# Storing the last step of a scan in eight half-tile stores on two issuing queues instead of two stores on one

## The chip, the cores and the metric

The kernel runs on one core of a Trainium2 chip. The metric is the time of one execution on the device, in microseconds (us). A core has a matrix engine (TensorE, PE in the profile, with its weight loads listed as PEld), a vector engine (VectorE, DVE), an activation engine (ScalarE, ACT), GpSimd (POOL), and SyncE (SP), which here only waits and issues transfers (DMAs). Each engine has its own instruction queue that it works through in order; engines wait for each other through semaphores. A DMA is issued by one engine's queue, carried out by 16 DMA engines, and counts 16 on a semaphore when it has landed.

## The reference

The input is x of shape (4, 512, 32, 48) in float32. It is group-normalised (32 groups of channels), and the result f is scanned over its last axis, forward and then backward, with one 512 by 512 matrix Wc (the centre tap of the convolution weight):

```
step(prev, x_i):  y = Wc @ prev + b;  y = where(y >= 0, y, a*y);  cur = y + x_i
fl  = forward scan over w = 0 .. 47        (47 steps after the first column)
out = backward scan over w = 46 .. 0       (47 steps, starting from fl[47])
result = x + out
```

So there are 94 dependent steps, each a 512x512 by 512x128 product (128 columns are 4 images by 32 rows) followed by a bias, a leaky ReLU and an addition. Column 0 of the output is known only after the last of them.

## The kernel before

The 512 channels are four tiles of 128 partitions. A step j computes four output tiles o = 0..3. For each, PE accumulates four matmuls (one per input tile k), 16 in all (L338, order in `UNITS`, so that tile o = 0 is finished before the others), ACT makes `above` = relu(z + b) (L406) and `below` = relu(-z - b) (L408), and DVE adds `above` to the state (L487, "part") and then subtracts a times `below` (L492, "whole"), which counts `state_ready`. The next step's matmuls wait for `state_ready` tile by tile.

In the backward half each finished column w gets the input added on DVE (L534 in the loop, L543 for columns 3, 2 and 1, which are written into places of `state` that are free) and is stored by SyncE, one DMA of 256 KB per column (L236), each after a wait on `out_ready`. The input of column 0 has been added ahead, before the backward half starts (L546), so the last step's tiles are final when L492 has run. That last step (`LAST_ORDER`) does part and whole of tile 0, then of tile 1, and so on.

Column 0 ("step 0" in the change) is stored in two pieces from SyncE: tiles 0 to 2 together after `state_ready` shows three tiles (L238, L239; 192 KB), tile 3 after the fourth (L240, L241; 64 KB). Then SyncE waits for the first three columns' stores (L242) and for all others (L243), and the kernel ends once every engine has met at the closing barrier (L59). The output tensor has the layout (W, 128, 4, 128): in column 0 a partition's four tiles are contiguous, 512 bytes each.

ACT issues one DMA in the whole kernel, at its start: the 2.5 KB of parameters (L349). Its 94 steps run in a loop (L401 to L411), after which its queue has nothing left but the closing barrier.

Of the kernel before, what the change touches and what calls it, by code (L numbers as in the profile page):

```python
# [9 lines left out]
P = 128  # L10
# [26 lines left out]
APART = 3  # L37
# [6 lines left out]

def scan_program(nc, x, w, par, out):
    KT, N, _, W, H = x.shape
    COLS = N * H
    FEAT = KT * COLS
    C = KT * P
    FWD = W - 1  # L50
    STEPS = 2 * FWD
# [7 lines left out]
    with ExitStack() as ctx:  # L59
        def sb(name, shape):  # L60
            return ctx.enter_context(nc.sbuf_tensor(name, shape, F32))

        def sem(name):
            return ctx.enter_context(nc.semaphore(name))

        xin = sb("xin", [P, KT, N, W, H])
        state = sb("state", [P, W, KT, COLS])
# [34 lines left out]
        def gmean(t):  # L102
            return gsums(t)[:, 0]

        def gvar(t):
            return gsums(t)[:, 1]

        def gdev(t):
            return spread(t, 4, P)[:, 0]
# [4 lines left out]
        def pieces(b):  # L114
            return PIECES.get(b, [W])
# [36 lines left out]
        state_ready = sem("state_ready")  # L152
        out_ready = sem("out_ready")
        input_added = sem("input_added")
        early_stored = sem("early_stored")
        stored = sem("stored")

        SROW, XROW = W * FEAT, NBLK * BLK

        def reg(eng, value, low, high):  # L160
            return value if isinstance(value, int) else eng.snap(value, min_val=low, max_val=high)
# [21 lines left out]
        def loop(eng, first, last, body):  # L183

            n = (last - first) // 2
            if n > 1:
                with eng.Fori(0, n) as turn:
                    for u in range(2):
                        body(turn * 2 + (first + u), (first + u) % 2)
                first += 2 * n  # L190
            for j in range(first, last):
                body(j, j % 2)

        def units(b):

            found = []
            begin = 0
            mine = BY_ACT.get(b, (0, 0))
            for i, size in enumerate(pieces(b)):
                w0 = begin  # L200
                begin += size
                while w0 < begin:
                    by_act = w0 == mine[0] and mine[1] > 0
                    w1 = mine[1] if by_act else w0 + UNIT
                    assert w1 <= begin
                    found.append((w0, w1, i, by_act))
                    w0 = w1
            return found

        def record(b, i):  # L210

            return sum(1 if by_act else 2 for _, _, _, by_act in units(b)[:i])

        def x_part(b, w0, w1):
            return xin[:, b // N, b % N, w0:w1, :].rearrange("p w h -> p (w h)")
# [7 lines left out]
        @block.sync  # L223
        def _(sp):
            for b in range(NBLK):
                w0 = 0
                for i, size in enumerate(pieces(b)):
                    sp.dma_start(xin[:, b // N, b % N, w0:w0 + size, :],  # L228
                                 x[b // N, b % N, :, w0:w0 + size, :]).then_inc(x_loaded[b][i], 16)
                    w0 += size  # L230
            for k in range(KT):
                sp.dma_start(w_t[:, k, :], w[k * P:(k + 1) * P, :]).then_inc(w_loaded[k], 16)
            for i in range(FWD):
                step = W - 1 - i
                sp.wait_ge(out_ready, i + 1)
                sp.dma_start(out[step], free[step] if step in free else state[:, step, :, :]).then_inc(  # L236
                    early_stored if i < APART else stored, 16)
            sp.wait_ge(state_ready, 4 * (STEPS - 1) + KT - 1)  # L238
            sp.dma_start(out[0, :, 0:KT - 1, :], state[:, 0, 0:KT - 1, :]).then_inc(stored, 16)  # L239
            sp.wait_ge(state_ready, 4 * STEPS)  # L240
            sp.dma_start(out[0, :, KT - 1, :], state[:, 0, KT - 1, :]).then_inc(stored, 16)  # L241
            sp.wait_ge(early_stored, 16 * APART)  # L242
            sp.wait_ge(stored, 16 * (FWD - APART + 2))  # L243

        @block.tensor
        def _(pe):
# [100 lines left out]
        @block.scalar  # L347
        def _(act):
            act.dma_start(params[:, :], par[:, :]).then_inc(params_loaded, 16)  # L349
            act.wait_ge(counts_set, 4)  # L350
            junk = state[:, W - 2:W, :, :].rearrange("p w k c -> p (w k c)")

            def unit_stats(nth):
                b = act_blocks[nth]
                i, (w0, w1, piece, _) = next((i, u) for i, u in enumerate(units(b)) if u[3])
                rec = bstat[:, b, record(b, i), :]
                size = (w1 - w0) * H
                act.wait_ge(x_loaded[b][piece], 16)
                nc.scalar.activation(junk[:, 0:size], x_part(b, w0, w1), ACT.Identity, scale=1.0 / size,  # L359
                                     accum_out=rec[:, 1:2]).then_inc(act_step, 1)  # L360
                act.wait_ge(act_step, nth + 1)
                nc.scalar.activation(junk[:, 0:size], x_part(b, w0, w1), ACT.Square, scale=-1.0, bias=rec[:, 1:2],  # L362
                                     accum_out=rec[:, 2:3]).then_inc(act_stats, 1)
                act.wait_ge(act_stats, nth + 1)

            def square_deviations(t):
                k, n0, n1 = BATCHES[t]
                act.wait_ge(dev_done, t + 1)
                nc.scalar.activation(dev2[:, k, n0:n1], gdev(t)[:, :, 0], ACT.Square).then_inc(dev2_done, 1)  # L369

            def group_values(t):
                k, n0, n1 = BATCHES[t]
                act.wait_ge(gvar_done, t + 1)
                nc.scalar.activation(var_eps[:, k, n0:n1], gvar(t)[:, :, 0], ACT.Identity,  # L374
                                     bias=eps[:, 0:1]).then_inc(var_done, 1)
                nc.scalar.activation(mean[:, k, n0:n1], gmean(t)[:, :, 0], ACT.Identity).then_inc(mean_kept, 1)

            unit_stats(0)
            act.wait_ge(params_loaded, 16)
            nc.scalar.mul(negative[:, :], params[:, :], -1.0).then_inc(negated, 1)  # L380
            unit_stats(1)
            unit_stats(2)
            square_deviations(0)
            group_values(0)
            unit_stats(3)
            unit_stats(4)
            square_deviations(1)
            group_values(1)
            unit_stats(5)
            unit_stats(6)  # L390
            square_deviations(2)
            group_values(2)
            unit_stats(7)
            unit_stats(8)
            square_deviations(3)
            act.wait_ge(gshift_done, 1)
            nc.scalar.activation(shift[:, :], gshift[:, :, 0], ACT.Identity).then_inc(shift_kept, 1)
            group_values(3)
            act.wait_ge(negated, 1)

            def body(j, par):  # L401
                nth = [reg(act, j * 4 + (o + 1), 1, 4 * STEPS) for o in range(KT)]
                for o in range(KT):
                    act.wait_ge(tile_done, nth[o])
                    z = psum[:, 4 * par + o, 0:COLS]
                    nc.scalar.activation(above[:, par, o, :], z, ACT.Relu, bias=params[:, o:o + 1],  # L406
                                         scale=1.0).then_inc(above_done, 1)
                    nc.scalar.activation(below[:, par, o, :], z, ACT.Relu, bias=negative[:, o:o + 1],  # L408
                                         scale=-1.0).then_inc(below_done, 1)

            loop(act, 0, STEPS, body)  # L411

        @block.vector
        def _(dve):
# [228 lines left out]
```

## Time and profile before

| | |
|---|---|
| median of 3 runs | 377.96 us (377.90 to 378.09) |
| profiled execution, its own time | 378.02 us |
| its span, first to last instruction | 376.5 us |
| PE busy in the span | 351.9 us (93%) |
| DVE, ACT busy | 287.2 us, 228.1 us |
| granted TensorE clock | 1.000 (2.4 GHz) |
| last state tile written | 374.24 us |
| last store issued, landed | 374.27 us, about 375.9 us |

The span is what the profile resolves; the 1.5 us between it and the execution's own time lie outside of any instruction. The chain of waits names, walking back from the last instruction, what released each piece of work. The DMA issue rows give the size of each DMA and the time from its issue to its landing.

### The profile page before, as it was taken

How to read it: one execution, taken by the hardware profiler on the slowest of the kernel's cores; microseconds unless marked ns; L12 is line 12 of the kernel's file. 1: busy time of each engine (PE TensorE's matmuls, PEld its weight loads, DVE VectorE, ACT ScalarE, POOL GpSimd, SP SyncE). 2: the span in 40 equal slices, each digit the busy share in tenths (PEclk: the TensorE clock that was granted, in tenths of full speed). 3: DMA queues.
4: the chain of work that ended last, by engine and by line, in shares of the span. 5: the costliest groups of instructions: out<-in, count | busy, mean ns of one | idle time of the engine just before them, and what ended most of it. 6: DMA issues, size and time to landing. Idle time of an engine off the chain costs nothing.

```text
span 376.5 us, 10084 instructions
## 1 busy us (share of the span) xinstructions
PE 351.9 (93%) x3096; PEld 350.3 (93%) x3096; DVE 287.2 (76%) x927; ACT 228.1 (61%) x803; POOL 19.3 (5%) x30
## 2 busy tenths in 40 slices
PE   0269999999999999999999999999999999999996
PEld 0169999999999999999999999999999999999995
DVE  2678997887888878655656778778778787787786
ACT  3765556566565565665665655656656656556564
POOL 2177000000000000000000000000000000000000
PEclk9999999999999999999999999999999999999999
DMA  7998000000000000000000112212212212122122
GB/s 304 423 412 311 2 0 0 1 0 0 1 0 0 1 0 0 0 0 0 0 0 0 57 67 74 84 56 84 84 56 84 78 62 84 64 76 84 56 111 84
DMA packets 10808, 26.30 MB, mean 70 GB/s; under 512 B 1328, under 2 KB 1584, under 8 KB 10800
## 3 DMA queue, kind: packets, MB, share of 16 engines
q1 hardware_dynamic: 10656, 26.22, 18.0%
q14 instruction: 6, 0.05, 0.0%
q8 instruction: 2, 0.03, 0.0%
q10 hardware_dynamic: 144, 0.00, 0.0%
HBM read 13.63 MB, written 12.58 MB: 70 GB/s over the span
## 4 chain that ended last, share of the span: by engine, by line
PE 90%; DMA 6%; SPq 2%; DVE 1%; ACT 0%; issue 0%; ACTq 0%
PE psum L338 88%; DMA xin<-in_x 6%; SPq L228 2%; PE psum L293 1%; PE psum L303 1%; DVE state L436 0%; DVE state L492 0%; DVE state L487 0%; ACT state L359 0%; PE psum L267 0%; ACT state L362 0%; PE psum L286 0%; ACT above L406 0%; PE psum L262 0%; PE psum L284 0%
## 5 line engine op out<-in xcount | busy, mean ns | idle before, releaser
L338 PE MATMUL psum<-state,w_t 128*128 (+1 forms) x2976 | 332.7, 275 | 0.0
L338 PEld LDWEIGHTS psum<-state,w_t 128*128 128x128 f32 x2976 | 332.5, 192 | 0.1
L406 ACT ACTIVATE above<-psum,params 128x128 f32<-128x128 f32 x376 | 140.1, 373 | 132.3 <-PE psum L338 128.8
L487 DVE TENSOR_TENSOR state<-above,state 128x128 f32 (+1 forms) x376 | 108.4, 288 | 66.7 <-ACT above L406 65.4
L408 ACT ACTIVATE below<-psum,negative 128x128 f32<-128x128 f32 x376 | 140.4, 374 | 0.0
L492 DVE SCALAR_TENSOR_TENSOR state<-below,negative,state 128x128 f32 (+1 forms) x376 | 123.6, 349 | 7.1 <-DVE state L487 0.2
L534 DVE TENSOR_TENSOR state<-state,xin (+1 forms) x45 | 30.8, 684 | 0.0
L418 DVE BATCH_NORM_STATS2 bstat<-xin 128x6 f32<-128x512 f32 x33 | 21.1, 678 | 12.3 <-DMA xin<-in_x 12.3
L436 DVE TENSOR_SCALAR state<-xin,mean,rstd 128x320 f32<-128x320 f32 (+3 forms) x73 | 28.6, 439 | 0.0
L254 PE MATMUL psum<-chan,centre 128*128 128x64 f32 (+1 forms) x8 | 2.0, 348 | 17.9 <-DVE chan L432 17.9
L254 PEld LDWEIGHTS psum<-chan,centre 128*128 128x128 f32 x8 | 1.6, 255 | 18.1 <-issue 13.5
L359 ACT ACTIVATE state<-xin 128x1024 f32<-128x1024 f32 (+1 forms) x9 | 8.2, 913 | 4.7 <-DMA xin<-in_x 4.6
L293 PE MATMUL psum<-same_group 128*128 128x128 f32 x56 | 9.3, 339 | 0.0
L362 ACT ACTIVATE state<-xin,bstat 128x1024 f32<-128x1024 f32 (+1 forms) x9 | 9.1, 1006 | 0.3
L293 PEld LDWEIGHTS psum<-same_group 128*128 128x128 f32 x56 | 9.0, 252 | 0.0
L596 POOL TENSOR_TENSOR state<-xin,mean 128x512 f32<-128x512 f32 x6 | 6.2, 1041 | 0.4
L601 POOL TENSOR_TENSOR state<-state,rstd 128x512 f32<-128x512 f32 x6 | 6.2, 1041 | 0.4
L586 POOL TENSOR_TENSOR rstd<-var_eps,minus_half 128x4 f32<-128x4 f32 (+2 forms) x5 | 4.5, 895 | 17.1 <-ACT var_eps L374 16.7
L267 PEld LDWEIGHTS psum<-dev,same_group 128*128 128x128 f32 x8 | 1.6, 249 | 3.6 <-ACT dev L369 3.6
L267 PE MATMUL psum<-dev,same_group 128*128 128x64 f32 (+1 forms) x8 | 2.3, 374 | 2.8 <-ACT dev L369 2.8
L359 ACT ACT_TABLE_LOAD x1 | 1.3, 1283 | 5.6 <-DMA xin<-in_x 5.6
L303 PE MATMUL psum<-state,w_t 128*128 128x128 f32 x32 | 4.2, 280 | 0.2 <-DVE state L436 0.2
(38 smaller groups left out, 26.2 us busy)
## 6 DMA issues: line engine op xcount, KB each, us to landing
out_y<-state SPq DMA_DIRECT2D x47, 256.0 KB, 2.0
xin<-in_x SPq DMA_DIRECT2D x13, 768.0 KB, 12.7
xin<-in_x SPq DMA_DIRECT2D x7, 256.0 KB, 17.7
w_t<-in_w SPq DMA_DIRECT2D x4, 256.0 KB, 10.3
xin<-in_x SPq DMA_DIRECT2D x1, 512.0 KB, 19.6
out_y<-state SPq DMA_DIRECT2D x1, 192.0 KB, 1.9
out_y<-state SPq DMA_DIRECT2D x1, 64.0 KB, 1.6
params<-in_par ACTq DMA_DIRECT2D x1, 2.5 KB, 4.9
```

What stands on the lines that cost most here:

```text
L293: nc.tensor.matmul(idle, same_group[:, :], same_group[:, :], start=True, stop=True)
L303: mm = nc.tensor.matmul(psum[:, o, 0:COLS], w_t[:, k, o * P:(o + 1) * P], state[:, 0, k, :], start=k == 0, stop=k == KT - 1)
L338: mm = nc.tensor.matmul(psum[:, 4 * par + o, 0:COLS], w_t[:, k, o * P:(o + 1) * P], xs[k], start=k == 0, stop=k == 3)
L359: nc.scalar.activation(junk[:, 0:size], x_part(b, w0, w1), ACT.Identity, scale=1.0 / size, accum_out=rec[:, 1:2]).then_inc(act_step, 1)
L362: nc.scalar.activation(junk[:, 0:size], x_part(b, w0, w1), ACT.Square, scale=-1.0, bias=rec[:, 1:2], accum_out=rec[:, 2:3]).then_inc(act_s ...
L406: nc.scalar.activation(above[:, par, o, :], z, ACT.Relu, bias=params[:, o:o + 1], scale=1.0).then_inc(above_done, 1)
L408: nc.scalar.activation(below[:, par, o, :], z, ACT.Relu, bias=negative[:, o:o + 1], scale=-1.0).then_inc(below_done, 1)
L418: return nc.vector.bn_stats(bstat[:, b, record(b, i):record(b, i) + 2, :].rearrange("p r v -> p (r v)"), x_part(b, w0, w1))
L436: return nc.vector.tensor_scalar(state[:, w0:w1, k, n * H:(n + 1) * H], xin[:, k, n, w0:w1, :], mean[:, k, n:n + 1], rstd[:, k, n:n + 1], ...
L487: nc.vector.tensor_tensor(sts[o], above[:, par, o, :], sts[o], ALU.add).then_inc(part_done, 1)
L492: nc.vector.scalar_tensor_tensor(sts[o], below[:, par, o, :], negative[:, KT:KT + 1], sts[o], ALU.mult, ALU.add).then_inc(state_ready, 1)
L534: return nc.vector.tensor_tensor(place, place, ready(dve, xin_step(dve, step)), ALU.add)
```

## The change

Column 0 is stored tile by tile. For each of its four tiles SyncE stores partitions 0 to 63 and ScalarE's queue stores partitions 64 to 127, each after a wait for that tile's `state_ready`. ScalarE's four waits and four DMAs come after its loop, so behind all of its activations, and count on a new semaphore, `last_stored`, for which SyncE waits at the end. No other engine's instructions change.

```diff
+        last_stored = sem("last_stored")
...
-            sp.wait_ge(state_ready, 4 * (STEPS - 1) + KT - 1)
-            sp.dma_start(out[0, :, 0:KT - 1, :], state[:, 0, 0:KT - 1, :]).then_inc(stored, 16)
-            sp.wait_ge(state_ready, 4 * STEPS)
-            sp.dma_start(out[0, :, KT - 1, :], state[:, 0, KT - 1, :]).then_inc(stored, 16)
+            for o in range(KT):
+                sp.wait_ge(state_ready, 4 * (STEPS - 1) + o + 1)
+                sp.dma_start(out[0, 0:P // 2, o, :], state[0:P // 2, 0, o, :]).then_inc(stored, 16)
             sp.wait_ge(early_stored, 16 * APART)
-            sp.wait_ge(stored, 16 * (FWD - APART + 2))
+            sp.wait_ge(stored, 16 * (FWD - APART + KT))
+            sp.wait_ge(last_stored, 16 * KT)
...
             loop(act, 0, STEPS, body)
+
+            for o in range(KT):
+                act.wait_ge(state_ready, 4 * (STEPS - 1) + o + 1)
+                act.dma_start(out[0, P // 2:P, o, :], state[P // 2:P, 0, o, :]).then_inc(last_stored, 16)
```

## Rows read from the trace of the kernel before

**Rows 1.** The page: span, busy time, and the chain that ended last

```profile
span 376.5 us, 10084 instructions
PE 351.9 (93%) x3096; PEld 350.3 (93%) x3096; DVE 287.2 (76%) x927; ACT 228.1 (61%) x803; POOL 19.3 (5%) x30
PE 90%; DMA 6%; SPq 2%; DVE 1%; ACT 0%; issue 0%; ACTq 0%
```

**Rows 2.** Chain of waits from 360 us: start us, us, what

```profile
359.97 11.40 PE psum L338 x102
...
371.40 0.38 ACT above L406
...
371.80 0.30 DVE state L487
...
372.13 0.35 DVE state L492
...
373.89 0.35 DVE state L492
```

**Rows 3.** Timeline, last step: start us, us, engine, line, what

```profile
371.42 0.33 SPq L236 DMA_DIRECT2D out_y<-state  x1
...
372.71 0.35 DVE L492 SCALAR_TENSOR_TENSOR state<-below,negative,state 128x128 f32<-128x128 f32 x1
...
373.23 0.36 ACT L408 ACTIVATE below<-psum,negative 128x128 f32<-128x128 f32 x1
373.30 0.35 DVE L492 SCALAR_TENSOR_TENSOR state<-below,negative,state 128x128 f32<-128x128 f32 x1
...
373.68 0.33 SPq L239 DMA_DIRECT2D out_y<-state  x1
...
374.27 0.33 SPq L241 DMA_DIRECT2D out_y<-state  x1
```

**Rows 4.** Closing lines: duration ns min/median/max, first and last start us

```profile
L243 SPq EVENT_SEMAPHORE  x1: 17/17/17, 375.9 to 375.9; - x1
...
L59 ACTq DRAIN  x1: 511/511/511, 373.1 to 373.1; - x1
...
L59 SPq EVENT_SEMAPHORE  x1: 17/17/17, 376.5 to 376.5; - x1
```

**Rows 5.** The page's DMA issues: count, KB each, median us to landing

```profile
out_y<-state SPq DMA_DIRECT2D x47, 256.0 KB, 2.0
...
out_y<-state SPq DMA_DIRECT2D x1, 192.0 KB, 1.9
out_y<-state SPq DMA_DIRECT2D x1, 64.0 KB, 1.6
params<-in_par ACTq DMA_DIRECT2D x1, 2.5 KB, 4.9
```

**Rows 6.** Windows: stretch, PE, PEld, DVE, ACT, POOL busy, PEclk, DMA share, GB/s

```profile
374.45:374.50 0.05, 0.00 (x0) 0.00 (x0) 0.00 (x0) 0.00 (x0) 0.00 (x0) 1.00 0.00 0
374.50:374.55 0.05, 0.00 (x0) 0.00 (x0) 0.00 (x0) 0.00 (x0) 0.00 (x0) 1.00 0.57 215
...
375.08:375.46 0.38, 0.00 (x0) 0.00 (x0) 0.00 (x0) 0.00 (x0) 0.00 (x0) 1.00 0.65 193
...
375.20:375.30 0.10, 0.00 (x0) 0.00 (x0) 0.00 (x0) 0.00 (x0) 0.00 (x0) 1.00 1.01 307
...
375.46:375.90 0.44, 0.00 (x0) 0.00 (x0) 0.00 (x0) 0.00 (x0) 0.00 (x0) 1.00 0.00 0
```

**Rows 7.** DMA issues by line: duration ns, start us (two lines' answers)

```profile
L228 SPq DMA_DIRECT2D xin<-in_x x1: 382/382/382, 0.8 to 0.8; - x1
...
L349 ACTq DMA_DIRECT2D params<-in_par x1: 404/404/404, 0.8 to 0.8; - x1
...
L236 SPq DMA_DIRECT2D out_y<-state x47: 332/332/347, 210.6 to 371.4; - x47
```

**Rows 8.** DMA queues in 1.0 to 2.4 us, and two windows as in rows 6

```profile
q10 hardware_dynamic: 2, 0.00, 0.1%
...
1.70:1.80 0.10, 0.00 (x0) 0.00 (x0) 0.00 (x0) 0.00 (x0) 0.03 (x2) 1.00 0.00 0
1.80:2.00 0.20, 0.00 (x0) 0.00 (x0) 0.00 (x0) 0.00 (x0) 0.20 (x1) 1.00 1.52 184
```

## The prediction

> **What bounds the kernel now.** I read the page's busy times and chain first, then the chain of waits near the end, the timeline of the last step, and windows over the last 2 us. The page [rows 1] shows a kernel that is bound by PE: 93% busy, 90% of the chain. The change touches none of that. It touches only what comes after the last matmul, so the question is how the chain ends. The chain [rows 2] leaves PE at 371.40 and runs through the last step's ACT and DVE work, tile by tile; its last compute piece is the fourth L492, 373.89 + 0.35 = 374.24. From there on nothing computes. The store of tile 3 is issued 0.03 us later, at 374.27 [rows 3], and lands 1.6 us after its issue [rows 5], at 375.87. SyncE's last wait then passes at 375.9, and the closing barrier ends the span at 376.5 [rows 4], 0.6 us later. The tail is therefore 0.03 + 1.6 + 0.6 = 2.26 us with rounding (376.5 - 374.24), and all of it lies behind the last state tile. The change can only alter this piece: 0.6% of the time.
>
> Inside the 1.6 us the windows [rows 6] show three parts. The 192 KB store, issued at 373.68, moves its first packets just after 374.50, that is 0.82 us after its issue. By the same delay the 64 KB store, issued at 374.27, starts at 374.27 + 0.82 = 375.09; it moves until about 375.46, 0.37 us; and from 375.46 to the landing at 375.87, 0.41 us, no DMA engine moves anything. Sum 0.82 + 0.37 + 0.41 = 1.60.
>
> **The change part by part.**
>
> The 192 KB store of tiles 0 to 2 goes, and becomes three pairs of 32 KB halves, issued as each tile is ready. In the last step's timeline the four L492 start at 372.13, 372.71, 373.30 and 373.89 [rows 2, 3], so the tiles are final at 372.48, 373.06, 373.65 and 374.24, 0.59 us apart. Such a pair is 64 KB, and needs 0.21 us of transfer at the best rate in the window of the last store (65.5 KB / 307 GB/s [rows 6]) to 0.37 us as that store took: less than the spacing either way. So no backlog stands in front of tile 3. What this takes off the path is small, because it was barely on it: the 192 KB store needs about 0.6 us from 374.50, so it was done by about 375.1, just as the 64 KB store started. Bounds: 0 to -0.05 us. I take -0.03.
>
> Tile 3 goes from one 64 KB store to two of 32 KB. Same bytes, same 512-byte rows, and the same 16 DMA engines if both halves are spread over all of them. The upper bound of the gain: the 0.37 us of transfer become the 0.21 us of the full rate, -0.16 us, if the slow build-up of the last store comes from rows being handed out one after another and two queues hand them out side by side. Also, if issuing 64 rows takes less than the 0.332 us that every 128-row store takes on SyncE [rows 7], some of the 0.82 us goes; at most half of 0.332, -0.17 us. Against it: the row gives 332 ns for 256 KB, and the 192 and 64 KB stores show 0.33 too [rows 3], so bytes don't matter to it; whether rows do isn't shown, since every one of them has 128. The lower bound of both is 0. I take -0.08 for the two together, nearer to zero, for want of any row with fewer partitions.
>
> SyncE's queue now issues four DMAs instead of two, at 372.51, 373.09, 373.68 and 374.27; 0.33 us each fits into the 0.59 us between them, so its fourth starts at 374.27 as before. Its first comes well after the column-1 store issued at 371.42 [rows 3], which has no issue left then.
>
> ScalarE's queue gets four waits and four DMAs, behind its last activation. Nothing of the kernel is queued behind them but the barrier, for which SyncE is later anyway. When can they start? The timeline has the last ACTIVATE from 373.23 to 373.59 [rows 3], but the closing drain on ACT's queue starts at 373.1 [rows 4], before that ACTIVATE does: the sequencer runs ahead of its engine. A DMA is the sequencer's work too, so the first should issue at about 373.1, tiles 0 and 1 being ready. With 0.332 us each (SyncE's rate [rows 7]) the issues stand at 373.10, 373.43, 373.76, and the fourth waits for its tile until 374.27. With 0.404 us each (ScalarE's only DMA, at the start [rows 7]) they stand at 373.10, 373.50, 373.91 and 374.31. So the lag is used up by the time tile 3 is final: 0 to +0.04 us; I take +0.02.
>
> Two queues issue at the same moment, 374.27. At the start of the kernel they do so too: SyncE's first load took 382 ns, ScalarE's 404 ns, both from 0.8 us [rows 7], against 332 alone. So side by side costs 0.05 to 0.07 us, if that is what the difference is; bounds 0 to +0.07, I take +0.05.
>
> The extra wait of SyncE on `last_stored` is one more 17 ns instruction behind the landing [rows 4]; bounds 0 to +0.05, I take +0.02.
>
> Sum: -0.03 - 0.08 + 0.02 + 0.05 + 0.02 = -0.02 us. The sum is made against the profiled execution's own 378.02 us (span 376.5 and 1.5 around it) and gives 378.00; that execution lies 0.06 above the median of 377.96, so against the median it is 377.94. I forecast 377.95, no change that can be told: the three runs alone span 0.19 us, and I count as a change only what exceeds 0.2%, 0.76 us.
>
> **A rule against the change.** The row [rows 7] shows two DMA issues that begin together at 0.8 us and both end within 0.41 us. Served strictly one behind the other at 0.332 us each, the later would have shown some 0.66 us. The Trainium skill, Perfetto Trace Analysis, section "DMA Instruction — HWDGE (DVE, Sync)", says otherwise: the block that writes the descriptors is shared by the two issuing sequencers, an issuer locks it for exclusive use, and the wait for the lock lies inside the DMA instruction's profiled time. By that rule the later of the two issues at tile 3 would end up to one issue later, and the backlog of ScalarE would count as well; the rival just below works out what that makes. The trace here speaks against a lock that lasts for the whole of an issue, but has only this one pair.
>
> **The rivals.**
>
> (A) Slower: the issues of both queues exclude each other. From 373.09 on there are three of SyncE's and four of ScalarE's left. One after another at 0.332 us they take 7 x 0.332 = 2.32 us and end at 375.41; before, the last issue ended at 374.27 + 0.33 = 374.60. The last landing comes 0.81 us later: 377.96 + 0.81 = 378.77, just over the 0.2%. It decides from about 0.32 us for each issue of a half; if 64 rows cost half, 0.166 us, seven of them are done by 374.25 and this costs at most 0.17 us. For it stands only the identical duration of every store; against it the pair at the start. Chance 0.07. This is the rule of the page named above, at its full price.
>
> (B) ScalarE's half lands late, but by less. Two ways. Its queue starts slowly: at the kernel's start SyncE's first packets move from about 1.8 us, 1.0 after issue, while the queue of ScalarE's DMA (q10) shows its first two packets only in a window that ends at 2.4, up to 1.6 after issue [rows 8]; the difference of 0.5 us may be a property of the queue, or of the 768 KB beside it. Or its DMA waits until its engine is empty, at 373.59: then the fourth issue is at 373.61 + 3 x 0.404 = 374.82, 0.55 us later. Either gives 378.4 to 378.5. Against the second stands the drain row. Chance 0.27, nine parts in ten of it under the 0.76 us.
>
> (C) Faster: halves are much cheaper to issue and the two streams fill the engines at once: -0.17 - 0.16, with nothing on the other side, 377.63. A gain over 0.2% would need the landing to come 0.85 us after issue, when start and the wait for the landing alone make 0.82 + 0.41. Chance 0.12.
>
> (D) That the change does not do what it says (both halves move but nothing gets shorter since the same 16 DMA engines move the same 512-byte rows) is what the forecast amounts to.
>
> **How the numbers follow.** Forecast 0.54, with its own range 377.8 to 378.2; A 0.07; B 0.27; C 0.12. The range from 377.65 to 378.5 holds the forecast, nearly all of C and most of B, about 0.84, and leaves out A and the late part of B. Slower by over 0.2%: all of A, somewhat above half since its price is just at the bound, so 0.05, and 0.03 from B: 0.08. Faster by over 0.2%: 0.01. Within: 0.91.
>
> **What would show it.** Right: the fourth issue on ScalarE's queue starts within 0.1 us of SyncE's, at some 0.03 us after the last L492; issues of 0.3 to 0.4 us on both; both halves of tile 3 land 1.5 to 1.65 us after issue; the first issue on ScalarE's queue starts ahead of its last ACTIVATE's end. A would show as issues of 0.5 us and more wherever the two queues overlap. B would show as a first issue after 373.6, or as a landing that takes 2 us and more on ScalarE's rows with SyncE's at 1.6. C would show as issues under 0.25 us. Wrong in the whole would be any change ahead of 371.4 us, for which I see no cause, as no instruction there changes, or a barrier that takes other than 0.6 us.

## The result, and the profile after

The change made the kernel slower: 379.38 us (median of 6, 379.27 to 379.40) against 377.93 (6 runs), a ratio of 1.0038 with the interval [1.0028, 1.0048]. That is 1.45 us, 1.9 times the 0.76 us that I had set as the least to count, and outside my range of 377.65 to 378.5.

The page of the changed kernel has the same work and the same chain shares on PE as [rows 1]; what differs is ScalarE's queue, q10, which carried 144 packets of 0.00 MB before and now carries 464 of 0.13 MB.

```profile
span 377.5 us, 10090 instructions
PE 352.2 (93%) x3096; PEld 350.6 (93%) x3096; DVE 286.9 (76%) x927; ACT 228.1 (60%) x803; POOL 19.3 (5%) x30
...
q10 hardware_dynamic: 464, 0.13, 0.2%
```

The timeline of its last step (start us, us, engine, line, what), which answers to [rows 3]:

```profile
371.24 0.33 SPq L237 DMA_DIRECT2D out_y<-state  x1
371.95 0.35 DVE L497 SCALAR_TENSOR_TENSOR state<-below,negative,state 128x128 f32<-128x128 f32 x1
372.33 2.71 SPq L241 DMA_DIRECT2D out_y<-state  x4
...
372.93 0.54 ACTq L416 DMA_DIRECT2D out_y<-state  x1
...
373.51 1.89 ACTq L416 DMA_DIRECT2D out_y<-state  x3
373.71 0.35 DVE L497 SCALAR_TENSOR_TENSOR state<-below,negative,state 128x128 f32<-128x128 f32 x1
```

The last state tile is final at 373.71 + 0.35 = 374.06; the whole step stands 0.18 us earlier than before, and most of that is there from the start: PE's first matmul begins at 13.36 us instead of 13.53. So times are best counted from that tile to the end of the execution, its tail. Before, 378.02 - 374.24 = 3.78 us. After, 379.27 - 374.06 = 5.21. All of the loss, 1.43 us, is in the tail. ScalarE's four issues run from 372.93 to 375.40, one behind the other, at about 0.6 us each. The rows of single issues and of the closing lines (duration ns min/median/max, first and last start us) answer to [rows 4, 7]:

```profile
L241 SPq DMA_DIRECT2D out_y<-state x1: 549/549/549, 372.3 to 372.3; - x1
DMA to landing us min/median/max: 1.9/1.9/1.9
...
L416 ACTq DMA_DIRECT2D out_y<-state x1: 540/540/540, 372.9 to 372.9; - x1
DMA to landing us min/median/max: 1.8/1.8/1.8
...
L416 ACTq DMA_DIRECT2D out_y<-state x1: 607/607/607, 374.8 to 374.8; - x1
DMA to landing us min/median/max: 1.9/1.9/1.9
...
L244 SPq EVENT_SEMAPHORE  x1: 28/28/28, 376.7 to 376.7; - x1
...
L59 SPq COMPARE_BRANCH  x1: 33/33/33, 377.2 to 377.2; - x1
...
L59 ACTq EVENT_SEMAPHORE  x1: 17/17/17, 377.5 to 377.5; - x1
```

L244 is SyncE's last wait, and the L59 rows are the closing barrier, of which SyncE's branch comes first. The reader is to see three things. The first half on SyncE, with nothing beside it (ScalarE's first comes 0.6 us later), takes 549 ns to issue where a whole tile of twice the bytes takes 332. ScalarE's last half starts at 375.40 - 0.61 = 374.79, 0.70 us after the 374.09 at which its tile allows it, and lands 1.9 us later instead of 1.6: 376.7. And from SyncE's last wait (376.7) to its next instruction (377.2) pass about 0.4 us; before, the wait [rows 4] and the branch both stand at 375.9:

```profile
L59 SPq COMPARE_BRANCH  x1: 33/33/33, 375.9 to 375.9; - x1
```

Sum 0.70 + 0.3 + 0.4 = 1.4 us.

### The profile page after: what moved, and what is told of

Its sections match the earlier page's. It is cut to its first block, busy times and chain, and to the rows that moved or that the text cites. A ratio compares the mean times of both kernels' runs of the same rounds, so it can differ in the third digit from the quotient of the medians.

```text
span 377.5 us, 10090 instructions
## 1 busy us (share of the span) xinstructions
PE 352.2 (93%) x3096; PEld 350.6 (93%) x3096; DVE 286.9 (76%) x927; ACT 228.1 (60%) x803; POOL 19.3 (5%) x30
## 4 chain that ended last, share of the span: by engine, by line
PE 90%; DMA 5%; SPq 2%; DVE 1%; ACT 1%; issue 0%; ACTq 0%
PE psum L339 88%; DMA xin<-in_x 5%; SPq L229 2%; PE psum L294 1%; PE psum L304 1%; DVE state L441 0%; DVE state L497 0%; DVE state L492 0%; ACT state L363 0%; ACT state L360 0%; PE psum L268 0%; PE psum L287 0%; ACT above L407 0%; PE psum L263 0%; PE psum L285 0%
```

## The experiments

Three theories at the start. **H**: a store of 64 partitions is dear in itself. **L**: the issues of two queues exclude each other (my rival A). **Q**: ScalarE's queue is slow (part of my rival B). **G** came from comparing the closing lines: one place in SyncE's instruction stream is passed late, whatever stands there.

### Whole tiles, halves from one queue, and ScalarE's queue alone

sp_tiles:

```diff
+            for o in range(KT):
+                sp.wait_ge(state_ready, 4 * (STEPS - 1) + o + 1)
+                sp.dma_start(out[0, :, o, :], state[:, 0, o, :]).then_inc(stored, 16)
```

> Column 0 in four whole tiles (128 partitions, 64 KB), all from SyncE. Three theories of where the change's 1.45 us come from. H: a store of 64 partitions is dearer than one of 128 (0.55 us of issue against 0.33, first packets 1.2 us after issue against 0.8), on whatever queue. L: the issues of the two queues exclude each other. Q: ScalarE's queue itself is slow or adds to the ending. None of the three is present here: all expect issues of 0.33 us, a landing 1.6 us after the last issue, and 377.9 us as before. If storing by tile costs in itself, this kernel shows it: three more 0.33 us issues can't all hide, and the time rises above 378.2.

sp_halves, the same loop with both halves in it:

```diff
+                sp.dma_start(out[0, 0:P // 2, o, :], state[0:P // 2, 0, o, :]).then_inc(stored, 16)
+                sp.dma_start(out[0, P // 2:P, o, :], state[P // 2:P, 0, o, :]).then_inc(stored, 16)
```

> The eight halves of the change, all from SyncE. H: eight issues of 0.55 us from 372.5 on, the last starting at about 376.3 instead of 374.3 and starting its packets 1.2 us later: about 380.3 us. L: one queue, so nothing excludes anything; issues of 0.33 us, the last 0.33 us after the first of tile 3: 378.2 to 378.4 us. Q: ScalarE issues nothing, so 377.9 to 378.4 us, and the stretch outside of the span is 1.5 us again.

act_last: 192 KB from SyncE as before, and tile 3 from ScalarE's queue, after its loop:

```diff
+            act.wait_ge(state_ready, 4 * STEPS)
+            act.dma_start(out[0, :, KT - 1, :], state[:, 0, KT - 1, :]).then_inc(last_stored, 16)
```

> As before (192 KB, then 64 KB, all partitions), but the 64 KB store of tile 3 is issued by ScalarE's queue. H and L: a whole store with nothing beside it, 0.33 to 0.40 us of issue, landing after 1.6 us: 377.9 to 378.0 us. Q: the landing takes 1.9 to 2.2 us and the stretch outside of the span grows from 1.5 to 1.75 us: 378.2 to 378.8 us.

Measured: whole tiles from SyncE 378.30 us (11 runs, ratio 1.0011 [1.0002, 1.0020]); eight halves from SyncE 381.22 (5 runs, 1.0087 [1.0073, 1.0101]); tile 3 from ScalarE's queue 377.90 (11 runs, 1.0000 [0.9991, 1.0009]).

Q falls: the store on ScalarE's queue, idle for 370 us, took 353 ns to issue and landed after 1.6 us. Halves are dear with a single queue in play, so L can't be the whole: 3.3 us lost, where L expected 0.5 at most. It is also 0.9 above what H expected, since back to back they are 0.64 us apart and not 0.55, and 0.4 us pass between two of them (the fifth's end, 375.62, and the sixth's start, 376.02) at the place that "The late instruction on SyncE" below is about. Its row for one line of halves (the timeline has them 0.64 us apart):

```profile
L240 SPq DMA_DIRECT2D out_y<-state x4: 549/591/604, 372.5 to 376.5; - x4
```

The whole tiles were a surprise. All four issues took 332 to 333 ns and landed after 1.6 us, yet the kernel lost 0.43 us. The profile of that kernel shows where, between SyncE's last wait and its branch, as in the change:

```profile
L242 SPq EVENT_SEMAPHORE  x1: 17/17/17, 375.8 to 375.8; - x1
...
L59 SPq COMPARE_BRANCH  x1: 33/33/33, 376.3 to 376.3; - x1
```

### Which stores are dear to issue

Columns of the middle are stored in pieces, off the path. forms, its first branch:

```diff
+                if step == 30:
+                    sp.dma_start(out[step, 0:64], state[0:64, step, :, :]).then_inc(stored, 16)
+                    sp.dma_start(out[step, 64:128], state[64:128, step, :, :]).then_inc(stored, 16)
```

> Off the path: five of the middle columns are stored in pieces from SyncE, one step apart, so that the issue of each form can be read by itself: column 30 as 64 + 64 partitions, 27 as 96 + 32, 24 as 112 + 16, 21 as tile 0 in 64 + 64 and the rest whole, 18 as tile 0, tile 1, tiles 2 to 3 with all partitions. The time stays 378 us. H: every piece of fewer than 128 partitions takes about 0.55 us to issue (or a time that follows the number of partitions), every piece of 128 takes 0.33 whatever its bytes. L: all take 0.33, since only one queue issues.

forms2 is the same with other cuts: 0:32, 0:16, 0:48, 0:80, 32:96, 0:96 and 0:64 as first pieces.

> Off the path: seven middle columns stored from SyncE in pieces of partitions, the first piece of each with nothing just ahead of it: 32, 16, 48, 80, 64 (partitions 32 to 95), 96 and 64. Expected: 96 takes 0.35 us and both pieces of 64 take 0.55, as in the run before. Should the issue follow the number of partitions, 80 lies between and 48, 32, 16 above 0.55; should 64 be an exception, the others take 0.33 to 0.35. Time 378 to 378.5 us, depending only on where the gap falls.

One run each, 378.08 and 378.03 us. First pieces, with nothing just ahead of them, in forms (64 partitions, 96, 112, then tile 0 in 64 and in 128 partitions):

```profile
L237 SPq DMA_DIRECT2D out_y<-state x1: 549/549/549, 271.2 to 271.2; - x1
...
L240 SPq DMA_DIRECT2D out_y<-state x1: 347/347/347, 281.9 to 281.9; - x1
...
L243 SPq DMA_DIRECT2D out_y<-state x1: 332/332/332, 292.6 to 292.6; - x1
...
L246 SPq DMA_DIRECT2D out_y<-state x1: 472/472/472, 303.3 to 303.3; - x1
...
L250 SPq DMA_DIRECT2D out_y<-state x1: 332/332/332, 314.1 to 314.1; - x1
```

and in forms2 (32, 16, 48, 80, then partitions 32 to 95; of the two that are not shown, 96 took 332 ns and 64 took 511):

```profile
L237 SPq DMA_DIRECT2D out_y<-state x1: 344/344/344, 271.2 to 271.2; - x1
...
L240 SPq DMA_DIRECT2D out_y<-state x1: 330/330/330, 282.0 to 282.0; - x1
...
L243 SPq DMA_DIRECT2D out_y<-state x1: 331/331/331, 292.7 to 292.7; - x1
...
L246 SPq DMA_DIRECT2D out_y<-state x1: 332/332/332, 303.4 to 303.4; - x1
...
L249 SPq DMA_DIRECT2D out_y<-state x1: 634/634/634, 314.1 to 314.1; - x1
```

The price follows neither the bytes nor the number of partitions. First pieces of 16, 32, 48, 80, 96, 112 and 128 partitions take 330 to 347 ns; those of 64 take 472 to 634, whether they start at partition 0 or 32 and whether a row has 512 or 2048 bytes. A piece right behind a piece of 64 takes 568 to 598 ns, right behind any other 421 to 433. So H holds in a narrower form: of the eight counts tried, all multiples of 16, only 64 is dear. Why 64, no run shows.

### Do the two queues exclude each other?

column_halves:

```diff
+                sp.dma_start(out[0, :, o, 0:COLS // 2], state[:, 0, o, 0:COLS // 2]).then_inc(stored, 16)
...
+                act.dma_start(out[0, :, o, COLS // 2:COLS], state[:, 0, o, COLS // 2:COLS]).then_inc(last_stored, 16)
```

> As the change (four issues on SyncE's queue, four on ScalarE's, each tile in two halves, the same waits), but a half is all 128 partitions and 64 of the 128 columns. H (a store of 64 partitions is dear to issue, in itself): issues of 0.33 to 0.45 us on both queues, the last on ScalarE's within 0.1 us of SyncE's at about 0.03 us after the last state tile, so 1.0 us of the change's 1.45 us are gone: 378.3 to 378.5 us, the ending's gap of 0.45 us staying. L (the queues exclude each other, whatever the form): issues of 0.6 us where they overlap, about 379.3 us.

Measured 378.42 us (11 runs, 1.0015 [1.0006, 1.0024]), as H has it. The rows of the two lines, SyncE's and ScalarE's:

```profile
L241 SPq DMA_DIRECT2D out_y<-state x4: 332/332/333, 372.3 to 374.0; - x4
L416 ACTq DMA_DIRECT2D out_y<-state x4: 363/443/444, 372.9 to 374.3; - x4
```

SyncE's issues don't lengthen at all beside ScalarE's. ScalarE's, back to back, come 0.48 us apart, so its fourth starts at 374.3 where the tile allows 374.05: a backlog of some 0.2 us remains, where I had expected 0.1 at most.

The packets in the trace of the change say the same of its halves of 64 partitions. ScalarE's first packets come 1.20, 1.26, 1.27 and 1.27 us after their issues; the first four halves of sp_halves, with one queue alone, have 1.20, 1.25, 1.26 and 1.25. So ScalarE's queue, which lands last, isn't held up by SyncE's. SyncE's is by ScalarE's: its second and third have 1.48 and 1.51, and its third took 835 ns to issue where no issue of sp_halves takes over 604. That is off the path, since ScalarE's last half lands later.

Then only the last tile, in halves of partitions (last_halves) and of columns (last_columns); tiles 0 to 2 in one store as before:

```diff
             sp.wait_ge(state_ready, 4 * STEPS)
-            sp.dma_start(out[0, :, KT - 1, :], state[:, 0, KT - 1, :]).then_inc(stored, 16)
+            sp.dma_start(out[0, 0:P // 2, KT - 1, :], state[0:P // 2, 0, KT - 1, :]).then_inc(stored, 16)
...
+            act.wait_ge(state_ready, 4 * STEPS)
+            act.dma_start(out[0, P // 2:P, KT - 1, :], state[P // 2:P, 0, KT - 1, :]).then_inc(last_stored, 16)
```

> Tiles 0 to 2 in one store from SyncE as before; only tile 3 in halves of 64 partitions, one from SyncE, one from ScalarE. SyncE's instruction count is that of the kernel before, so no gap at the end, and ScalarE has no backlog. H: both issues take 0.55 us instead of 0.33, both halves land 1.9 us after issue instead of 1.6: 378.1 to 378.2 us, so that 0.3 us is what the form costs once. L: one issue of 0.33 and one of 0.66 us or more, 378.2 us as well, told by the durations.

> The same, but tile 3 in two halves of 64 columns with all 128 partitions. H: issues of 0.33 and 0.36 us, landing after 1.5 to 1.6 us: 377.8 to 377.9 us, at most 0.1 us below the kernel before. L: one of the two issues takes 0.66 us: 378.2 us.

Measured 378.54 us (11 runs, 1.0018 [1.0008, 1.0027]) and 378.12 (11 runs, 1.0008 [0.9999, 1.0017]), some 0.4 and 0.3 us above the middle of what I expected. The issues in last_halves were 549 and 557 ns, in last_columns 333 and 371, so both at once and at their own price. But ScalarE's half landed later than SyncE's: 2.1 against 1.8 us, and 1.8 against 1.6. The view of the queues over 40 slices of 374 to 377 us (0.075 us each) of last_halves shows it as two humps behind the 192 KB, the second beginning where the first ends (SyncE's packets move from 375.38 to 375.68 us, ScalarE's from 375.65 to 375.95):

```profile
GB/s 0 0 0 0 0 102 307 328 348 389 410 348 267 123 0 0 0 0 61 164 157 62 102 198 110 21 0 0 0 0 0 0 0 0 0 0 0 0 0 0
```

In last_columns ScalarE's packets (375.13 to 375.44) overlap SyncE's, which end at 375.32, and still land later. So L holds in part. With one exception, SyncE's 835 ns above, the issue as the profile shows it isn't prolonged, but of two stores issued at one instant the second lands 0.2 to 0.3 us later, with 64 partitions nearly one whole transfer behind the first. The Trainium skill, Perfetto Trace Analysis, "DMA Instruction — HWDGE (DVE, Sync)", has the unit that writes descriptors used by one issuer at a time and puts the wait for it inside the profiled duration. The order of the two humps agrees with the first; the unchanged durations of 549 and 557, and of 333 and 371 ns, don't agree with the second, and only the 835 ns could.

### The late instruction on SyncE

Waits on loads that landed long ago are put ahead of SyncE's column stores, where it idles for 180 us (n is 8, 2 or 16 in the kernels below):

```diff
+            for b in range(n):
+                sp.wait_ge(x_loaded[b][0], 16)
             for i in range(FWD):
```

> The changed kernel with eight waits more on SyncE, on loads that landed long ago, ahead of its first column store, where SyncE is idle for 180 us. G: in the change and in the whole tiles from SyncE, 0.45 us pass between SyncE's last wait and its next instruction, in the kernel before less than 0.1; it depends on how many instructions stand ahead on SyncE (72 loads and stores and the four of column 0, with their waits), and moving the place to where SyncE waits anyway hides it: 378.9 to 379.0 us, 0.4 below the change. Without G, if the gap belongs to the work that was just done: 379.4 us or slightly more.

> Whole tiles from SyncE (378.30 us, 0.43 above the kernel before) with the same eight waits ahead. G: the gap of 0.45 us at the end is hidden, 377.85 to 377.9 us, the same as before or a little below it. Without G, if storing by tile costs 0.43 us in itself: 378.3 us.

> The kernel before with two such waits ahead, which brings SyncE's last instructions to the same count as in the kernel that stores whole tiles. G: the gap appears in a kernel that does nothing else differently, 378.3 us. Without G: 377.9 us.

Measured: the change with 8 waits 379.01 us (7 runs, 1.0030 [1.0019, 1.0042]); whole tiles with 8 waits 377.97 (11 runs, 1.0001 [0.9992, 1.0010]), 0.33 below the same kernel without them; the kernel before with 2 waits 378.23 (11 runs, 1.0009 [1.0000, 1.0018]). Instructions that do nothing made two kernels faster and one slower, as G has it. The intervals reach about 0.35 us to either side, as much as these differences, so the weight lies on two other things: the single runs do not overlap (378.87 to 379.19 against 379.27 to 379.40, 377.82 to 378.05 against 378.26 to 378.35, 378.12 to 378.56 against 377.76 to 378.08), and the closing rows show the gap itself come and go. In the last one the gap has moved by one instruction, to between branch and drain:

```profile
L59 SPq COMPARE_BRANCH  x1: 33/33/33, 375.8 to 375.8; - x1
L59 SPq DRAIN  x1: 82/82/82, 376.3 to 376.3; - x1
```

> The kernel before with eight waits ahead of SyncE's column stores. G, and a fixed place in SyncE's instruction stream: the place is passed while SyncE waits for columns, so nothing shows, 377.9 us. If instead any waits more on SyncE cost 0.4 us at the end, as two of them did, 378.3 us or more.

That expectation missed: 378.41 us (11 runs, 1.0015 [1.0006, 1.0024]). Counting SyncE's records (the instructions that its trace lists; two empty waits make one) from 0 in each trace gave the reason. In 14 of the 17 traces record 79 starts 0.39 to 0.42 us after the end of record 78, whatever it is: the last semaphore of the barrier in the kernel before, the branch in the change, the drain with 2 waits (81 records instead of 80), and here, with 84 records, the very store of tile 3. Of the other three, act_last has no record 79, and in forms and forms2 it is a column store that waits for its column until 2.8 and 3.2 us after record 78, so a gap of 0.4 us couldn't show. The store of tile 3 was issued 0.16 us after its tile instead of 0.03 and landed after 1.9 us instead of 1.6, which is 0.4 of the 0.57 us lost:

```profile
L243 SPq DMA_DIRECT2D out_y<-state x1: 332/332/332, 374.2 to 374.2; - x1
DMA to landing us min/median/max: 1.9/1.9/1.9
```

The kernel before has the late record too, in SyncE's 376.5 against 376.2 for the other engines' last semaphores, but nothing is lost by it: the kernel with tile 3 on ScalarE's queue, with 79 records and so without a record 79, has the same time. A place that moves with the count can be put where SyncE waits anyway:

> The kernel before with sixteen waits ahead of SyncE's column stores (eight cost 0.55 us, against what I expected). Theory G2: in every trace so far SyncE's instruction number 79, counted from 0 over the trace's records, comes about 0.4 us late, whatever it is; with eight waits more (four records) it was the last store. Sixteen waits (eight records) bring it to the store of column 3, three steps ahead of the end, and hide it: 377.9 us, 0.5 below the kernel with eight. If waits cost in themselves, 378.4 us or more.

377.89 us (11 runs, 0.9999 [0.9990, 1.0008]): sixteen waits cost nothing where eight had cost 0.57 us.

One thing in the traces moves with the place. Queue q14, whose kind the profile calls "instruction", moves a last packet of 8 KB that starts 1.0 to 1.6 us after the end of record 78 in all seventeen traces, forms, forms2 and act_last too; its other packets behind 50 us stay where they are within half a microsecond. In 376.5 to 378 us of the kernel before, and in 365 to 367 us of this one, where record 79 is the store of column 3:

```profile
q14 instruction: 1, 0.01, 1.9%
...
q14 instruction: 1, 0.01, 1.4%
```

That suggests that the late record sits where SyncE's instructions are fetched. No run shows it: the packet starts after the late record has run, at 377.12 against 376.49 in the kernel before, and can't be what that record waited for.

### Both causes taken away

split_96_32:

```diff
-                sp.dma_start(out[0, 0:P // 2, o, :], state[0:P // 2, 0, o, :]).then_inc(stored, 16)
+                sp.dma_start(out[0, 0:96, o, :], state[0:96, 0, o, :]).then_inc(stored, 16)
...
-                act.dma_start(out[0, P // 2:P, o, :], state[P // 2:P, 0, o, :]).then_inc(last_stored, 16)
+                act.dma_start(out[0, 96:P, o, :], state[96:P, 0, o, :]).then_inc(last_stored, 16)
```

> The change with 96 partitions on SyncE and 32 on ScalarE in place of 64 and 64. H2: only pieces of 64 partitions are dear to issue (0.51 to 0.63 us against 0.33 to 0.35 for 16, 32, 48, 80, 96, 112 and 128). Issues of 0.33 to 0.35 us on SyncE, 0.36 and then 0.44 on ScalarE, last landings about 1.8 us after the last tile; the late instruction 79 stays where it is in the change: 378.3 to 378.5 us, 0.9 to 1.0 below the change. If splitting partitions costs in itself, 379.4 us.

> The same with sixteen waits ahead on SyncE, so that instruction 79 is passed at column 3: both causes taken away. 377.9 to 378.1 us, the kernel before within 0.2; a third cause would show as what is left above that.

Measured 378.60 us (11 runs, 1.0018 [1.0009, 1.0027]) and, with the sixteen waits, 378.20 (11 runs, 1.0007 [0.9998, 1.0016]), each 0.1 above what I expected at most. Their single runs don't overlap (378.45 to 378.80 against 378.05 to 378.30). The rows of split_96_32:

```profile
L241 SPq DMA_DIRECT2D out_y<-state x4: 316/322/347, 372.6 to 374.3; - x4
L416 ACTq DMA_DIRECT2D out_y<-state x4: 372/432/435, 373.2 to 374.5; - x4
```

The sum of the change's 1.45 us by these kernels, each against the kernel before as timed beside it (377.93 beside the change, 377.88 beside these two): 1.45 - 0.72 = 0.73 for the 64 partitions, 0.72 - 0.32 = 0.40 for the late record, and 0.32 left. In the trace of the kernel with both taken away ScalarE's last issue starts at 374.4 against SyncE's 374.2, so about 0.2 of the 0.32 is its backlog of issues 0.48 us apart; the other 0.1 I can't place by a row. No version beat the kernel before: the best with another storing pattern are tile 3 on ScalarE's queue (377.90) and whole tiles with the late record hidden (377.97), both the same as before.

## Why the prediction was wrong

- That the change touches only the tail was right; all 1.43 us are there.
- The backlog in front of tile 3 was worth nothing measurable: whole tiles with the late record hidden are at 377.97.
- **The step that failed is the price of a half's issue**: "at most half of 0.332, -0.17 us ... The lower bound of both is 0". I let fewer rows make it cheaper or leave it, never dearer, though I had written that every row in the trace has 128 partitions. It was +0.2 to +0.3 us for each issue: 540 to 612 ns (SyncE's third took 835, off the path), 0.64 us from one to the next on a queue. The uncovered side of that bound is where the result lay.
- It struck hardest in the next step, "the lag is used up by the time tile 3 is final". ScalarE's first issue came when I said, ahead of its last ACTIVATE (372.93 against 373.05 to 373.41), so the second way of rival B, which waits for an empty engine, did not occur. But four issues at 0.62 us end at 375.40 and not at 374.7. Even at the price of a whole store back to back, 0.47 to 0.48 us apart rather than the 0.332 of a lone one, 0.2 us of lag would have been left. I had taken the price of stores 3.6 us apart for stores in a queue.
- "Two queues issue at the same moment", bounds 0 to +0.07: the issues' durations fit when only tile 3 was split, the landing of the second did not: 0.2 to 0.3 us later. In the change itself the two last halves were issued 0.37 us apart, and this price doesn't show.
- "The extra wait", bounds 0 to +0.05: the wait itself is cheap (SyncE's one closing record for its waits takes 28 ns instead of 17). What I had no term for is that SyncE's two stores more moved its late record from the end of the barrier to the branch that the barrier waits for: 0.4 us. It is why the barrier took 0.80 us from SyncE's last wait to the end of the span, not the 0.6 that I had called a sign of being wrong. The 0.4 us between SyncE's last two closing rows stood in the profile before, and I read past it.
- Rival A named the right place (a backlog of issues on ScalarE's queue, 378.77) with the wrong reason. A queue by itself is that slow with halves of 64 partitions, as eight halves from SyncE show.

## What to carry to other kernels

Splitting the last store shortened nothing in any version here: of the 1.6 us in the kernel before, 0.8 pass from issue to first packet and 0.4 from last packet to landing, halves of 64 partitions take 1.2 to their first packet, and each further DMA adds its own issue. Take the price of an issue from stores of the same number of partitions and the same distance, and where the trace has none, leave both sides of the bound open. When a difference of 0.3 to 0.5 us at the end has no cause in the work, compare the last records of each queue and shift them with a few empty waits before believing any explanation.

## What the runs showed of the hardware that I had not expected

- A store of 64 partitions with nothing just ahead of it takes 472 to 634 ns to issue, and one of 32 KB landed 1.8 to 1.9 us after its issue; 16, 32, 48, 80, 96, 112 or 128 partitions take 330 to 347 ns, and whole tiles of 64 KB landed after 1.6. Other counts were not tried.
- A second issue right behind another on SyncE's queue takes 421 to 433 ns, behind one of 64 partitions 568 to 598.
- Of two stores issued at one instant on the two queues, ScalarE's landed 0.2 to 0.3 us after SyncE's, with hardly any trace of it in the issues' durations (333 and 371, 549 and 557 ns).
- Record 79 of SyncE's stream starts no sooner than 0.39 us after the end of record 78, whatever instruction it is; moving it by empty waits was worth -0.33, -0.37 and -0.40 us, or +0.38 where it met the drain and +0.57 where it met the last store. An 8 KB packet of kind "instruction" follows the end of record 78 by 1.0 to 1.6 us in every trace; what holds record 79 up was not found.
- ScalarE's queue, idle for 370 us, issues and lands a store like SyncE's (353 ns, 1.6 us).
